# The second image's conv inputs, a difference and the last conv group in other slots of a hand-written slot order

## The reference

```python
x = L0(x)   # channel attention of each image: softmax(max - q q^T) q, then a squeeze gate: se*x + (1-se)*out
x = L1(x)   # 1x1 reduce, 3x3 depthwise, relu, attention over channels in the Fourier domain, gate, 1x1 post, + x
x = L2(x)   # group norm, 8-head attention over the 256 pixels of an image, projection, + x
# L3: the stage with the convolutions that the change is about
q, k, v = conv3x3(x, Wq), conv3x3(x, Wk), conv3x3(x, Wv)
att  = softmax(einsum('nchw,mchw->nmhw', q, k) / sqrt(C), axis=1)     # over the 16 images, pixel by pixel
virt = einsum('nmhw,mchw->nchw', att, v)
x    = x + conv3x3(relu(layernorm(virt) * gamma + beta), Wc)
```

## Time and profile before

| what | us |
|---|---|
| median of 3 runs | 499.03 (496.84 to 500.08) |
| profiled execution | 500.01 |
| its span, first to last instruction | 498.2 |
| PE busy in it | 465.4 |
| DVE busy | 344.7 |
| ACT busy | 249.3 |
| POOL busy | 126.4 |

### The profile page before, as it was taken

How to read it: one execution, slowest core, us unless ns; L and a number is a source line. 1 busy time by engine, 2 the same in 40 slices (tenths; PEclk the granted TensorE clock), 3 DMA queues, 4 the chain that set the end, 5 groups by cost and what they waited for, 6 DMA issues and landing times.

```text
span 498.2 us, 10552 instructions
## 1 busy us (share of the span) xinstructions
PE 465.4 (93%) x3790; PEld 374.0 (75%) x3790; DVE 344.7 (69%) x890; ACT 249.3 (50%) x590; POOL 126.4 (25%) x154
## 2 busy tenths in 40 slices
PE   7999999988998999899899989999996999998896
PEld 6877765767586778677776867777774789898895
DVE  1448578867687787788777876876476442776895
ACT  3424756645555555555556455534633431294551
POOL 6022443474012112201120121120110011332762
PEclk9999999898899999999999999999997999998998
DMA  7100012030001001000100000000000000005112
GB/s 271 45 22 2 1 49 91 1 91 23 0 6 44 18 0 42 21 0 0 42 21 0 12 9 0 2 23 1 0 1 22 1 22 2 1 1 168 44 50 77
DMA packets 10639, 15.28 MB, mean 31 GB/s; under 512 B 624, under 2 KB 8944, under 8 KB 10480
## 3 DMA queue, kind: packets, MB, share of 16 engines
q1 hardware_dynamic: 10608, 14.86, 9.3%
HBM read 10.66 MB, written 4.19 MB: 30 GB/s over the span
## 4 chain that ended last, share of the span: by engine, by line
PE 71%; DVE 13%; ACT 6%; issue 4%; POOL 3%; DMA 1%; DVEq 0%; SPq 0%; ACTq 0%; POOLq 0%
PE bank L1232 10%; PE bank L1233 8%; PE bank L1234 8%; PE bank L1345 5%; PE bank L1437 5%; PE bank L1374 5%; PE bank L1411 3%; PE bank L1239 3%; PE bank L1409 2%; PE bank L1465 2%; PE bank L1452 2%; PE bank L1249 2%; DVE nmax L1007 1%; PE bank L1261 1%; PE bank L1297 1%
## 5 line engine op out<-in xcount | busy, mean ns | idle before, releaser
L1232 PE MATMUL bank<-win,w_hi 128*128 128x256 f32 x384 | 117.2, 305 | 2.6 <-POOL win L592 1.2
L1233 PE MATMUL bank<-win,w_hi 128*128 128x256 f32 x384 | 108.9, 284 | 0.0
L1234 PE MATMUL bank<-win,w_lo 128*128 128x256 f32 x384 | 108.7, 283 | 0.0
L751 ACT ACTIVATE prob<-bank 128x512 f32<-128x512 f32 x128 | 69.5, 596 | 69.7 <-PE bank L1409 69.0
L1007 DVE TENSOR_REDUCE nmax<-bank 128x2 f32<-128x512 f32 x128 | 84.9, 687 | 18.8 <-PE bank L1374 18.4
L1232 PEld LDWEIGHTS bank<-win,w_hi 128*128 128x128 f32 x384 | 73.1, 190 | 9.5 <-issue 1.6
L1233 PEld LDWEIGHTS bank<-win,w_hi 128*128 128x128 f32 x384 | 73.3, 191 | 0.4
L1234 PEld LDWEIGHTS bank<-win,w_lo 128*128 128x128 f32 x384 | 73.1, 190 | 0.0
L540 POOL TENSOR_TENSOR first<-first 128x256 f32<-128x256 f32 x24 | 17.7, 737 | 152.7 <-ACT first L643 152.7
L1239 PE MATMUL bank<-ones_r 128*128 128x256 f32 x276 | 50.0, 319 | 1.1 <-DVE ones_r L856 1.1
L1374 PE MATMUL bank<-qk 32*128 32x256 f32 x256 | 33.0, 335 | 12.7 <-DVE nmax L1007 7.2
(11 more groups left out here) (240 smaller groups left out, 900.0 us busy)
## 6 DMA issues: line engine op xcount, KB each, us to landing
w_stage<-convs SPq DMA_DIRECT2D x4, 576.0 KB, 4.0
x_t<-x_px SPq DMA_DIRECT2D x8, 256.0 KB, 3.1
x_in<-x SPq DMA_DIRECT2D x8, 256.0 KB, 2.8
out<-x_pair SPq DMA_DIRECT2D x8, 256.0 KB, 2.2
q<-out SPq DMA_DIRECT2D x1, 2048.0 KB, 8.4
out<-v SPq DMA_DIRECT2D x8, 256.0 KB, 2.1
cst<-small SPq DMA_DIRECT2D x1, 1712.0 KB, 9.1
cst<-small SPq DMA_DIRECT2D x1, 253.5 KB, 3.5
```

The lines of the kernel that those rows point to most:

```text
L751: act.activation(prob[:, x // 4 % 2, x % 4, :, :], bank[ST_BANK[x % 2]][:, :], ACT.Exp, scale=L2_SCALE).then_inc(st_exp, 1)
L1232: mm(dst, hi, x_hi, start=(row == 0), stop=False)
L1233: mm(dst, hi, x_lo, start=False, stop=False)
L1234: return mm(dst, lo, x_hi, start=False, stop=(row == KH - 1))
```

## The change

Five entries of the slot tables change; no instruction is added or taken away. `diff0` moves from slot 12 to 14 in POOL's order. The six units of the last group leave slot 6: three stay there and three go to slot 9. The third join goes from slot 8 to slot 12. The windows of the second image go from slot 10 to 11 (in slot 11 they come behind the maximum). The high parts of the two images go from slots 8 and 11 to 10 and 12, the low parts from 11 and 12 to 11 and 13.

```diff
-POOL_SLOTS = {"rn": 1, "squares": 8, "diff0": 12, "grstd": 18}
+POOL_SLOTS = {"rn": 1, "squares": 8, "diff0": 14, "grstd": 18}
-CONV_NEXT = (6, 0, 0, 6, 0, 0, 6, 0, 0, 0, 0, 0, 0, 0, 0, 0, 0, 0, 0, 0, 0, 0, 0, 0)
+CONV_NEXT = (6, 0, 0, 6, 0, 0, 3, 0, 0, 3, 0, 0, 0, 0, 0, 0, 0, 0, 0, 0, 0, 0, 0, 0)
-JOIN_SLOTS = {1: SLOTS + 2, 2: SLOTS + 8}
+JOIN_SLOTS = {1: SLOTS + 2, 2: SLOTS + 12}
-WINDOW_SLOTS, ADD_SLOT, RESIDUAL_SLOT, HIGH_SLOTS, LOW_SLOTS = (3, 10), 6, 7, (8, 11), (11, 12)
+WINDOW_SLOTS, ADD_SLOT, RESIDUAL_SLOT, HIGH_SLOTS, LOW_SLOTS = (3, 11), 6, 7, (10, 12), (11, 13)
```

## The result

| what | before | after |
|---|---|---|
| median | 499.00 us (496.84 to 500.08) | 520.83 us (519.19 to 525.13) |
| profiled execution | 500.01 | 520.77 |
| its span | 498.2 | 519.0 |
| mean granted clock | 0.974 | 0.966 |

The ratio of after to before is 1.0452, 95% interval 1.0415 to 1.0489 (the two medians by themselves give 1.0437). Every run timed here was in the faster of the two states that executions come in but one of the kernel of experiment 6, at 527.84 us, which is left out. The forecast was 520 us, in a range of 510 to 530, through PE held at slot 11 and coming back at a lower clock.

A forecast was written before the change was run, and what follows sets the result against it. PE bounds the kernel, busy 43.95 of a 45.60 us block. Hold 14.0, clock 7.5, pair 1's block +1.0 and pair 7's -1.0 sum to 21.5, giving 520.5 against the median 499.03; forecast 520 us, range 510 to 530.

The forecast's parts named there:

- The hold: At slot 11's fillers PE waits 4.0 us for the third join, in five blocks, pairs 2 to 6.
- forecast 14.0 + 1.0 - 1.0: Loss without the clock: 14.0 us from five held blocks, +1.0 in pair 1's block, -1.0 in pair 7's.
- forecast 7.5: PE comes back from the wait at half clock: 1.5 us a block, the middle of 0 to 3, five times.
- forecast of 2.8: Lateness per held block at slot 13's conv, 2.85 us, taken as 2.8 in five blocks.
- held, but at full clock: Rival, chance 0.17: same wait at slot 11, but the low-clock stretches fall into it; 513 us.
- faster: Rival, chance 0.04: the join isn't last at slot 11, maximum 11 alone releases slot 12; 489 us.
- The 0.49 of the second low part: Slot 13's conv waits 0.49 us more a block, its low part now behind att_n, gate and maximum 13.
- Gain 0.70 a block, by itself: Splitting the last group brings slot 8's exponentials earlier and fills slot 10's wait for ACT: 0.70 us a block.
- the 2.36: Slot 12 starts 2.36 us late in a held block, gains at slots 10 and 12 already included.
- Pair 1's block: No join wait there; the low part comes 2.1 us later, about 1.0 of it hidden: +1.0 us.
- Pair 7's block: PE isn't held; slot 12's wait for maximum 11 shrinks, the conv waits instead: -1.0, between -2.2 and +1.
- diff0 ahead of DVE: Rival, chance 0.14: POOL's diff precedes DVE's first low part, delaying it and the join up to 1.27 us; 525 us.

The follow-up runs named there:

- experiment 6: The changed kernel with diff0 back in slot 12 of POOL's order: 520.17 us, ratio 1.0427 to the kernel before.
- experiment 2: The changed kernel with 28 more filler matmuls into bank 1 ahead of the wait for the join: 513.0 us, ratio 1.0278 to the kernel before.
- experiment 1: The changed kernel with slot 11's fillers writing an unread half of bank 1, waiting for slot 9's logit, not the joins: 509.11 us.
- Experiment 7: The changed kernel with the second low part back in slot 12, ahead of att_n, gate and maximum 13: 519.99 us.
- experiment 9: The kernel before with the last group split over slots 6 and 9, join in slot 10 at the earliest, first high part in slot 10: 502.72 us.
- experiment 5: The changed kernel with the third join in slot 10 instead of 12, the earliest the split group allows: 511.85 us.
- experiment 3: The kernel before with only the third join moved, from slot 8 to slot 12: 526.54 us, ratio 1.0567.
- experiment 4: The kernel before with only the second image's windows in slot 11 and the high parts in 8 and 12: 492.72 us, ratio 0.9875.
- experiment 8: The kernel of experiment 4 without slot 11's two filler matmuls and their wait: 492.85 us, ratio 0.9883 to the kernel before.

## Why the prediction was right

The mechanism, its place and the size were those of the forecast; some terms were off by tenths of a microsecond a block, partly in opposite directions.

- *The hold.* Forecast: PE idle for 4.0 us ahead of line 1239, five times. It is 3.81 to 3.82, five times. The join's end comes 4.5 us after slot 10 (line 1049's pair starts at 257.95, PE goes on at 258.75), against 249.39 - 244.75 = 4.6. The steps of the earlier trace rows that make the chain kept their lengths in the new order, so the chain could be added up.
- *Hold and clock in money.* With the clock kept up the loss is 14.0 us (experiment 2), forecast 14.0 + 1.0 - 1.0; the clock costs 7.8, forecast 7.5. By the loop's blocks the hold is 2.67 a block for a forecast of 2.8, and the clock 1.91 for 1.5 (five times the two would be 22.9, and 21.8 was measured). That the totals meet the forecast to a few tenths is therefore partly luck: in pair 1's block, for one, after was at 0.50 for 3.4 us where before was for 6.8, which the sum had not counted. The rival "held, but at full clock" (513) had the price of that kernel to the microsecond, but the case itself did not come.
- *That the two were additive was not clear.* Taking the wait away gives back 11.7, not 14 + 7.8, because the second low part is late by itself and the clock still falls behind the wait for it (experiment 1). The prediction saw that wait only as 0.49 us behind the hold, and its rival "faster" supposed that without the hold slot 12 would set the pace and 489 come out. It was the conv of slot 13 that did: 509, with the clock at half speed for a while in three of the five blocks besides.
- *The 0.49 of the second low part* holds for a PE at full clock. With nothing to wait for, the conv starts 0.25 behind the matmul ahead of it (250.93 to 251.18 in the kernel before); in experiment 2 it starts 0.71 behind it (257.85 to 258.56), which is 0.46 more. In after it is 0.58 in pair 4's block, so 0.33, and in the other four blocks the low part was done before the conv's turn, since PE at half speed arrives late itself (pair 3: low part done at 213.98, conv at 215.07). Experiment 7 resolves no loss from it.
- *"Gain 0.70 a block, by itself"* of the split doesn't stand by itself: the group's join has to follow it, into the stretch where DVE is what slot 12 waits for (experiment 9). In the sum it made no error, since the 2.36 was counted from the join.
- *Pair 1's block*: conv 7.14 after slot 10 (104.09 to 111.23), before 6.51 (103.59 to 110.10): +0.6 for a forecast of +1.0, released by line 1036 as it said. *Pair 7's block*: the wait for maximum 11 is gone, and the conv waits 2.49 for the second low part instead. The delay goes from 21.3 us at 391.94 (line 1465) to 20.6 at the conv: -0.8, forecast -1.0. Part of that is the clock of the kernel before, which was at 0.50 there from 379.7 to 386.5: its values at 382.03 took 1.93 us, those of after at 400.89 took 1.07.
- *diff0 ahead of DVE* did not happen: the low part starts at 257.01, POOL's diff at 257.13, and the low part keeps its 0.68. The order is the forecast one, by 0.12 us (0.10 to 0.12 in the four blocks) where the prediction had 0.2. att_n then takes 0.29, no longer 1.10. In experiment 5, where the diff starts amid the windows, the hold-up of DVE is there, 1.1 us. The Trainium skill ("SBUF - State Buffer", Who interferes with whom) has DVE and GpSimd share a port pair as an exclusive lock; both rows agree with it, though line 409, which starts 0.02 us behind the diff by the profile, still took its 0.27. So little decided it that the 0.14 was not too high.

What decides how long PE stays at the lower clock is open. In after the stretch at 0.50 lasted 6.8 us in pair 3's block (207.5 to 214.4) and 3.4 in pair 4's (258.7 to 262.1), behind the same wait of 3.8; the block that holds the longer one is 50.79 long, the next 49.67. The prediction's 1.5 a block was a middle between bounds, not a derivation, and experiment 3, with 2.4, shows that it could have been off by 4 to 5 us in all.

## What to carry to other kernels

Before something is moved back in one engine's queue, look for everyone who waits for it, down to matmuls whose result nobody reads: two fillers here held a whole PE queue, because the bank they write was still to be read. A change of several entries is worth taking apart: of this one, the windows behind maximum 11 are a gain of 1.2% alone (some of it perhaps the clock's, see below), and the join's place costs more than four times that. And a stall of the matmul engine should be priced as the wait plus the slow stretch behind it; where the wait can't go, work that keeps the engine busy in it gave back 7.8 of 21.8 us here.

## What the runs showed of the hardware

- The price of one and the same stall isn't fixed. In pair 1's block PE waits for line 959 (1.35 to 1.52 us) in all these kernels. Behind it the granted clock was 0.50 from 120.2 to 127.1 in the kernel before, from 122.2 to 125.6 in after, and never fell in the kernels of experiments 2, 3, 4 and 8. The windows of 1 us right behind this wait, in after and then in the kernel of experiment 4:

```profile
122.00:123.00 1.00, 1.00 (x11) 0.86 (x7) 0.93 (x5) 0.71 (x2) 0.00 (x0) 0.59 0.06 16
123.00:124.00 1.00, 1.00 (x7) 1.00 (x6) 0.80 (x4) 0.38 (x1) 0.71 (x1) 0.50 0.00 0
```

```profile
121.00:122.00 1.00, 1.00 (x12) 0.85 (x13) 1.00 (x2) 0.00 (x0) 0.58 (x1) 1.00 0.07 16
122.00:123.00 1.00, 1.00 (x9) 1.00 (x10) 0.90 (x6) 0.99 (x2) 0.00 (x0) 1.00 0.00 0
```

  The same holds in experiment 1: a wait of 1.9 us in each block, and the clock fell to 0.50 for some 7 us in the block of pair 3 (206.2 to 213.0), not in pair 4's; conv to conv the two are 49.04 and 46.27 us long. The Trainium skill ("TensorE: Matmul & The Clock Gate", Part 1: The HAM clock gate) says that how many matmuls run cold at a kernel's start varies from run to run of one kernel; here the slow stretch varied between places of one run too. Some 2.8 us of the 6.9 by which the profiled run of experiment 4 is faster lie in pair 1's block (from this wait to slot 10 of pair 2's block, 34.33 against 31.50), so part of its gain may hang on this; the 0.68 of each loop block does not.
- The longest waits were the surest: of the five of 3.8 us in after and the five of 3.7 in experiment 3, behind each the clock was at 0.50 for a while.
- Matmuls that nobody reads, run in place of the wait, kept the clock at 1.00 through all of 249 to 259 (experiment 2).
- DVE and POOL: one 0.28-us instruction took 1.39 under POOL's diff (experiment 5), and in experiment 4 a low part took 1.07 instead of 0.68 under the same diff (244.97 to 246.53). It ended at 247.08, and the conv behind it started at 247.14, 0.37 behind the matmul ahead of it instead of 0.25: 0.12 lost. The join's two instructions ran beside the diff in after at their usual length (0.41 and 0.75).
